# Reciprocal roots of the norms: one power operation on GpSimd in place of eight steps on VectorE, in a kernel whose order is planned

## The reference

```
var = jnp.mean(jnp.square(x), axis=-1, keepdims=True)
return x * jax.lax.rsqrt(var + EPS) * w
```

## Time and profile before

| | |
|---|---|
| median of 3 runs | 2589.81 us (2587.14 to 2590.7) |
| profiled execution, its own time | 2590.26 us |
| its span, first to last instruction | 2588.1 us |
| TensorE busy | 2476.7 us, 96% |
| VectorE busy | 1507.4 us, 58% |
| ScalarE busy | 1265.0 us, 49% |
| GpSimd busy | 990.7 us, 38% |
| mean granted TensorE clock | 0.989 |

### The profile page before, as it was taken

How to read it: one execution, slowest core, us unless ns; L and a number is a source line. 1 busy time by engine, 2 the same in 40 slices (tenths; PEclk the granted TensorE clock), 3 DMA queues, 4 the chain that set the end, 5 groups by cost and what they waited for, 6 DMA issues and landing times.

```text
span 2588.1 us, 53863 instructions
## 1 busy us (share of the span) xinstructions
PE 2476.7 (96%) x20277; PEld 1484.9 (57%) x20277; DVE 1507.4 (58%) x3448; ACT 1265.0 (49%) x4274; POOL 990.7 (38%) x994
## 2 busy tenths in 40 slices
PE   6999989999999999999999999999999999999998
PEld 3546555656565655565656564656655555566564
DVE  2536647767344755766644474767744456476763
ACT  2336526547242654564534364556544347274562
POOL 0024345656110434565411151654621034265452
PEclk9999999999999999999999999999999999999999
DMA  7000022112210002111210101112121010211112
GB/s 207 1 22 18 12 76 59 30 56 57 74 50 25 10 3 65 50 30 50 79 57 19 33 2 50 30 44 61 30 79 58 2 33 2 61 31 42 50 31 70
DMA packets 156154, 113.81 MB, mean 44 GB/s; under 512 B 30804, under 2 KB 153464, under 8 KB 155768
## 3 DMA queue, kind: packets, MB, share of 16 engines
q1 hardware_dynamic: 151440, 110.04, 14.7%
q10 hardware_dynamic: 4456, 0.29, 0.2%
HBM read 101.87 MB, written 8.42 MB: 43 GB/s over the span
## 4 chain that ended last, share of the span: by engine, by line
PE 76%; DVE 10%; ACT 7%; issue 3%; POOL 2%; ACTq 1%; DMA 0%; SPq 0%; DVEq 0%; POOLq 0%
PE bank L1446 10%; PE bank L1463 5%; PE bank L1077 5%; ACT Ebuf L1558 5%; PE bank L1163 5%; PE bank L1351 4%; PE bank L1360 4%; PE bank L1332 4%; PE bank L1339 4%; PE bank L1386 3%; PE bank L1452 3%; PE bank L1139 2%; PE bank L1312 2%; PE bank L1323 2%; PE bank L1296 2%
## 5 line engine op out<-in xcount | busy, mean ns | idle before, releaser
L1961 POOL TENSOR_TENSOR Ebuf<-Ebuf,row_rcp 128x512 f32<-128x512 f32 (+1 forms) x328 | 342.9, 1049 | 826.4 <-DVE row_rcp L1784 825.5
L1763 DVE TENSOR_REDUCE minus_max<-bank 128x8 f32<-128x512 f32 (+1 forms) x328 | 219.8, 673 | 96.5 <-PE bank L1139 75.0
L1558 ACT ACTIVATE Ebuf<-bank,minus_max 128x64 f32<-128x64 f32 x800 | 239.4, 333 | 17.0 <-DVE minus_max L1763 15.9
L1567 ACT ACTIVATE PT<-bank 128x512 f32<-128x512 f32 (+1 forms) x328 | 190.7, 610 | 99.1 <-PE bank L1163 97.8
L1163 PE MATMUL bank<-ident,Ebuf 128*128 128x128 f32 x1296 | 198.3, 281 | 14.2 <-POOL Ebuf L1961 11.1
L1163 PEld LDWEIGHTS bank<-ident,Ebuf 128*128 128x128 f32 x1296 | 146.7, 144 | 69.8 <-issue 50.5
L1558 ACT ACTIVATION_READ_ACCUMULATOR Ebuf<-bank,minus_max 128x1 f32 x800 | 180.9, 226 | 0.0
L1446 PE MATMUL bank<-xs_b,w_ring 128*128 128x512 f32 (+1 forms) x384 | 172.7, 613 | 2.5 <-DVE xs_b L1854 2.1
L1446 PE MATMUL bank<-xs_a,w_ring 128*128 128x512 f32 (+1 forms) x384 | 168.3, 600 | 1.8 <-POOL w_ring L2012 1.8
L1784 DVE RECIPROCAL row_rcp<-row_sum 128x8 f32<-128x8 f32 (+1 forms) x328 | 65.4, 201 | 112.4 <-ACT Ebuf L1558 106.8
L1768 DVE TENSOR_TENSOR Ebuf<-bank,minus_max 128x512 f32<-128x512 f32 x160 | 110.7, 692 | 16.6
(11 more groups left out here) (334 smaller groups left out, 5583.4 us busy)
## 6 DMA issues: line engine op xcount, KB each, us to landing
w_ring<-differences SPq DMA_DIRECT2D x70, 384.0 KB, 3.5
w_ring<-in_L_W SPq DMA_DIRECT2D x64, 256.0 KB, 2.9
w_ring<-in_L_l_gate SPq DMA_DIRECT2D x80, 128.0 KB, 3.3
w_ring<-in_L_l_up SPq DMA_DIRECT2D x80, 128.0 KB, 3.1
w_ring<-in_L_l_down SPq DMA_DIRECT2D x80, 128.0 KB, 3.2
differences<-w_ring SPq DMA_DIRECT2D x10, 384.0 KB, 2.9
arena_a<-in_x SPq DMA_DIRECT2D x4, 512.0 KB
arena_b<-in_x SPq DMA_DIRECT2D x4, 512.0 KB
```

The lines of the kernel that those rows point to most:

```text
L1558: last = A(Ebuf[:, u % UNITS, cell], bank(token)[:, cell], ACT.Exp, bias=minus_max[:, u % UNITS, c:c + 1], scale=query_scale(st, key) if k ...
L1567: A(PT[:, t % PTS, 0:width(key) * S], bank(token)[:, 0:width(key) * S], ACT.Copy).then_inc(pt_ready, 1)
L1763: V.reduce_max(minus_max[:, u % UNITS, 0:g], cells(bank(token)[:, 0:g * S]), AX_X, negate=True).then_inc(maxed, 1)
L1961: G_.tensor_tensor(v, v, row_rcp[:, n % 3, 0:g].unsqueeze(2).broadcast_to([P, g, S]), ALU.mult).then_inc(probs_ready, 1)
```

## The change

The eight steps behind the eviction are taken out. VectorE's eviction now writes var + eps itself, and GpSimd raises it to the power -0.5 with one tensor_tensor operation, whose second input is a column of -0.5 (filled once at the start). So the token "sums" has a third engine, and GpSimd's queue has 104 instructions more. The planner's entry for "sums" changes from 1.8 on VectorE to 0.25 on VectorE and 0.3 on GpSimd; LOADED changes from 10 to 6. room gets two conditions: g and qk with last index 0 are placed only once GpSimd's part of their norm's spread has been placed, and down only once GpSimd's part of its u has. All engines' orders and the numbers of fillers are computed anew from this.

```diff
-LOADED = 10.0
+LOADED = 6.0
 ...
     if step == "sums":
-        return chain(("PE", 0.42 if n in HALVED else 0.85), ("DVE", 1.8))
+        return chain(("PE", 0.42 if n in HALVED else 0.85), ("DVE", 0.25), ("POOL", 0.3))
 ...
+def early_norm(step, n):
+
+    return (3 * n - 1, 1) if step == "g" else (3 * n - 3, 0)
 ...
     def room(token):
-        key = where[0] if where else None
+        key, last = (where[0], where[-1]) if where else (None, None)
         if step == "weigh":
             return slot()
+        if (step in ("g", "qk") and last == 0 and (("spread", s, turn, *early_norm(step, key)), "POOL") not in end
+                or step == "down" and (("u", *token[1:]), "POOL") not in end):
+            return None
 ...
-                    V.tensor_scalar(w, bank(token)[:, 0:some.stop - some.start], -0.5 * RSQRT_UNIT / D, -0.5 * RSQRT_UNIT * eps, ALU.mult, ALU.add
+                    V.tensor_scalar(st.var[:, some], bank(token)[:, 0:some.stop - some.start], 1.0 / D, eps, ALU.mult, ALU.add
                                     ).then_inc(var_ready[s].sem, 1)
-                    dve.wait_ge(*var_ready[s].at(turn, RUN[n, h] + 1))
-                    V.tensor_scalar(y.bitcast(I32), w.bitcast(I32), -0.5, RSQRT_SEED, ALU.mult, ALU.add).then_inc(rsqrt_step[s].sem, 1)
...
-                    V.scalar_tensor_tensor(out=y, in0=step_a, scalar=1.875 / RSQRT_UNIT, in1=y, op0=ALU.add, op1=ALU.mult
-                                           ).then_inc(rstd_ready[s].sem, 1)
 ...
+            G_.memset(minus_half, -0.5).then_inc(s_half, 1)
+            pool.wait_ge(s_half, 1)
 ...
+                if step == "sums":
+                    n, h = where
+                    some = slice(2 * h, 2 * h + 2) if n in HALVED else slice(0, PAIRS)
+                    pool.wait_ge(*var_ready[s].at(turn, RUN[n, h] + 1))
+                    G_.tensor_tensor(st.rstd[:, some], st.var[:, some], minus_half.broadcast_to([P, some.stop - some.start]), ALU.pow).then_inc(rstd_ready[s].sem, 1)
```

More of the change, by code:

```diff
@@ L34 @@
 EPS_RMS, EPS_LN = 1e-6, 1e-5
-RSQRT_UNIT = 1.5 ** (1 / 7)
-RSQRT_SEED = float(0x5F3759DF - (1 << 30) - 3843802)
 SLOTS = 4
@@ L698, in xattn_kernel @@
     turn_sign = small[:, 4:5]
+    minus_half = small[:, 5:6]
     ident = sb("ident", [P, P])
@@ L731, in xattn_kernel @@
         st.media_raw = raw[:, :].bitcast(U8).rearrange("p (a s) -> p a s", s=S)
-        norm = sb(f"norm_{x}", [P, 16])
-        st.minus_half_var, st.rstd, st.step_a, st.step_b = (norm[:, k * PAIRS:(k + 1) * PAIRS] for k in range(4))
+        norm = sb(f"norm_{x}", [P, 2 * PAIRS])
+        st.var, st.rstd = norm[:, 0:PAIRS], norm[:, PAIRS:2 * PAIRS]
         st.arena = sb(f"arena_{x}", [P, 7168])
@@ L770, in xattn_kernel @@
     s_ident, s_const, s_setup, s_table = sem("s_ident"), sem("s_const"), sem("s_setup"), sem("s_table")
-    s_types, s_early, s_blank = sem("s_types"), sem("s_early"), sem("s_blank")
+    s_types, s_early, s_blank, s_half = sem("s_types"), sem("s_early"), sem("s_blank"), sem("s_half")
     s_tanh, s_tiled = sem("s_tanh"), sem("s_tiled")
@@ L790, in xattn_kernel @@
     runs = len(NORM_RUNS)
-    var_ready, rsqrt_step, rstd_ready = pair("var_ready", runs), pair("rsqrt_step", 7 * runs), pair("rstd_ready", runs)
+    var_ready, rstd_ready = pair("var_ready", runs), pair("rstd_ready", runs)
     x0_ready, normed = pair("x0_ready", 2), pair("normed", 4)
@@ L1805, in _ @@
                     n, h = where
-                    k = 7 * RUN[n, h]
                     some = slice(2 * h, 2 * h + 2) if n in HALVED else slice(0, PAIRS)
-                    w, y, step_a, step_b = (v[:, some] for v in (st.minus_half_var, st.rstd, st.step_a, st.step_b))
                     dve.wait_ge(*filled(token))
                     eps = EPS_LN if n in (1, 2) else EPS_RMS
-                    V.tensor_scalar(w, bank(token)[:, 0:some.stop - some.start], -0.5 * RSQRT_UNIT / D, -0.5 * RSQRT_UNIT * eps, ALU.mult, ALU.add
+                    V.tensor_scalar(st.var[:, some], bank(token)[:, 0:some.stop - some.start], 1.0 / D, eps, ALU.mult, ALU.add
```

## The result

The changed kernel takes 2562.35 us (median of five runs, 2560.15 to 2563.82). Beside it the kernel before took 2587.14 us on five runs (2578.72 to 2590.7), the ratio is 0.990 with a 95% interval of 0.988 to 0.992: faster by 1.0%. The forecast was 2566. The profiled execution took 2560.15, its span is 2558.3, 29.8 less than the span before.

What follows compares the result with a forecast made beforehand. TensorE, busy 96% of the span, bounds the kernel; only its 193 us of idle time and fillers can be won. Terms 17 + 5 + 4 - 1 - 1 = 24 us gave 2566 us, range 2546 to 2589, likeliest case 2557 to 2574.

Steps and rivals of the forecast that it cites:

- The uncovered norms: Seventeen norms where TensorE waits between sums and spread with latency uncovered: gap 0.84 in place of 1.84 us, 17 us gained.
- P: Assumed duration of one GpSimd power operation, taken as 0.4 us, with 0.10 and 1.06 as ends.
- the power operation is dear: Rival: GpSimd needs much longer for a power than a product, 1.06 us, giving 2582 us; chance 0.16.
- The disturbed norms: Norms whose VectorE steps stretch beside GpSimd work, holding 11 us of TensorE idle time: 5 gained, ends 0 and 9.
- rows 9: Profile rows near 2443 us: L1814 took 0.69 us inside a GpSimd operation read as 2.02 us; TensorE idled 1.56.
- VectorE's relief: Work queued behind the eight steps on VectorE comes up to 1.6 us earlier: 4 us gained, -6 to +16.
- the moved waits: Power operation waiting in GpSimd's queue delays probabilities and transposes, 1 us lost; new conditions in room, 1 us; LOADED 0.
- The signs named: Profile checks: 104 operations averaging 0.3 to 0.5 us, gap near 0.85, some 340 fillers, spread waits below 12 us.
- a rival as slower: Between L1296 and L1305, from P = 1.40 uncovered norms are longer than now; at P = 2, 2606 us; chance 0.09.
- clock case: Rival: gaps without fillers lower TensorE's granted clock by 0.01, 2600 us at worst; chance 0.06, shared with a poor order.

## Why the prediction came out right, and which of its terms did not

The direction, the range and the time hold: 24 us forecast, 24.8 measured between the medians. That the two agree so closely is partly luck. Between the profiled executions, from which the terms below are read, the gain is 29.8 us, and the terms missed in both directions: the first gave 5 us less than forecast, the others together 11 us more.

**The uncovered norms: 17 us forecast, 12.2 measured** (33.8 to 21.6 us). The place, the count, the three fillers and the free GpSimd were as read. The term mis-sized is P: I took 0.4 from the price per column of a product; it is 0.70 and 1.01. The upper end, 1.06, held for both shapes in all but the disturbed operations, of which the longest took 1.49. The case "the power operation is dear", 2582 at P = 1.06, had the right price and the wrong time, for it gave nothing to the terms that follow.

**The disturbed norms: 5 forecast, 8.8 measured** (11.0 to 2.2 us). With the eight steps in the new order such places idle for 8.9 us again, in 12 norms, and with the power operation for 1.2 us in three, so most of this term belongs to the operation and not to the order. My reading of rows 9 took two GpSimd operations of 2.02 us together for one.

**VectorE's relief and the order, less the moved waits: 4 - 2 = 2 forecast, 8.8 left over** (29.8 - 12.2 - 8.8). This is a rest and not a measurement; some 3 us of clock and the 2.5 us between two executions of one program are in it. The run with eight idle products behind each eviction puts the relief itself at 10 us. I had looked for it in TensorE's waits for VectorE; what can be seen of it goes from minus_max through the exponentials and GpSimd's probabilities, and through the clock. VectorE did not fall to 1311 but to 1336 us, as rope's addition (L1907, L1892 now) got slower, from 86 to 101 us; that the busier GpSimd did it is not shown.

**The moved waits: -2 forecast, not measured by themselves.** No new wait for w_ring (3.7 us in one place, as before), 11.9 us for the probabilities; the conditions cost nothing that can be measured, and LOADED changes no instruction.

**The signs named.** 104 operations, but with a mean of 0.84 in place of 0.3 to 0.5 us; the gap 1.34 and 1.03 in place of 0.85; fillers 344 (forecast 340); waits of the spread 9.2 (below 12). GpSimd rose by 89 us and not by 42, with P.

**What the prediction did not see** is how steep the kernel is in this latency. It counted a rival as slower from P = 1.40, from the gap alone. Doubling P cost 46 us at a mean of 0.84, since further norms come uncovered and the clock falls. As an estimate, a straight line through the two puts the break-even with the kernel before at a mean P of about 0.84 + 25 / 55 = 1.3 us. The steps in the new order, a chain of 1.73 us, are 36 us slower than the kernel before. The prediction's clock case had no working behind its "2600 at worst": 1% of TensorE's 2477 us is 25. The runs have 30 us more of busy time for a clock lower by 0.011 (the steps in the new order). The Trainium skill's rule (GPSIMD Engine Reference, section 4.1, Engine selection), that elementwise work belongs on VectorE, is about one operation on either engine. No run has a power on VectorE; against one of VectorE's steps of 0.16 us, which is less work, the power took four times as long with two columns and six times with four. For the kernel the measurement decides the other way, because one instruction took the place of eight.

## What to carry to other kernels

A chain of small dependent instructions costs at two places, as latency where nothing covers it and as load on an in-order queue where others wait behind it; an expensive single operation on an idle engine can win both. Where a planner orders the work, try more than one figure for the new operation in the plan: the same program text gained 25 us with a guess of 0.3 us, 42 us with the measured 0.7 and 1.0, and as much with figures half way, so the measured duration is a good start but was not shown to be the cause. The reverse, a chain of eight steps that is much longer than planned, lost 36 us. And before a gap is called harmless, ask what TensorE's clock does behind it.

## What the runs showed of the hardware

- A tensor_tensor power on GpSimd takes 0.70 us for 128x2 and 1.01 us for 128x4 (up to 1.49 us where it is disturbed), where GpSimd's product of 128x512 takes 1.06 us.
- Small VectorE instructions on SBUF operands that take 0.16 us alone took 0.69 us beside a GpSimd operation.
- Idle pieces of 0.7 to 1.5 us, with matmuls between them, were followed by half clock, 1.2 GHz; with fillers in the planned waits the mean granted clock of the kernel was 0.990, without them 0.955.
- The length of one idle piece does not settle it: behind the wait of 3.63 us for a chunk the clock was 1.00 over the next 3.7 us, and behind the same wait, 3.67 us, in the changed kernel it was 0.55.
- Two profiles of one program differ by 2.5 us of span, at mean clocks of 0.990 and 0.992.
